# Two stage heads of a long kernel: the first attention's first operands asked for during the projection, the experts' spare rows on another queue

## The reference

```python
x = x + _L0_attn_ref(_layernorm(x), ...)
#   qkv = x @ W_attn + b_attn;  16 heads of 16
#   att = softmax(q k^T / sqrt(16) + alibi and causal mask);  y = att @ v;  y @ W_proj + b_proj
x = x + _L0_ffn_ref(...)
x = x + _L1_attn_ref(...)
x = x + _L1_ffn_ref(_layernorm(x), ...)
#   logits = xt @ w_router;  top1 = argmax;  slot = top1 * C + position, C = 160
#   buf[slot] = xt;  y = (silu(buf @ w_gate) * (buf @ w_up)) @ w_down;  out = xt + y[slot] * gate
```

## Time and profile before

| | us |
|---|---|
| median of three runs | 3570.31 (3567.07 to 3571.28) |
| the profiled execution | 3574.62 |
| span from its first to its last instruction | 3572.8 |
| PE busy in the span | 3193.6 (89%) |
| DVE, ACT, POOL busy | 2458.4, 1846.8, 1411.3 |
| mean granted TensorE clock | 0.953 |

### The profile page before, as it was taken

One profiled execution on the slowest core, in us unless ns is written; L12 is line 12 of the kernel. 1 busy time (PEld: TensorE's weight loads), 2 busy tenths in 40 slices (PEclk: granted clock), 3 DMA queues, 4 the chain that ended last, 5 costly groups with the idle time before them and its releaser, 6 DMA issues. The chain is left out here.

```text
span 3572.8 us, 52196 instructions
## 1 busy us (share of the span) xinstructions
PE 3193.6 (89%) x18048; PEld 1967.1 (55%) x18048; DVE 2458.4 (69%) x4614; ACT 1846.8 (52%) x3942; POOL 1411.3 (40%) x967
## 2 busy tenths in 40 slices
PE   8599999979999989999999899898388888888878
PEld 5244444346666645566666555433156555555777
DVE  8488887647777632277777433379699999999543
ACT  2177767736666611156666311165467777777111
POOL 4201111132222211132222211133499999999433
PEclk9699999989999999999999899999599999999989
DMA  5945657110020043000020123134444252420776
GB/s 165 168 57 91 88 86 133 35 35 23 23 66 23 14 171 99 26 19 24 22 67 21 37 68 91 48 138 149 164 170 177 82 177 86 173 93 36 260 264 219
DMA packets 263746, 347.27 MB, mean 97 GB/s; under 512 B 70619, under 2 KB 183241, under 8 KB 262844
## 3 DMA queue, kind: packets, MB, share of 16 engines
q1 hardware_dynamic: 249572, 308.29, 31.0%
q10 hardware_dynamic: 9432, 23.35, 1.9%
q0 software_dynamic: 4480, 12.30, 0.9%
HBM read 227.72 MB, written 112.80 MB: 95 GB/s over the span
## 5 line engine op out<-in xcount | busy, mean ns | idle before, releaser
L2411 POOL TENSOR_TENSOR H_feed<-H_ndu,H_bs 128x1024 f32<-128x1024 f32 x256 | 595.0, 2364 | 6.1 <-DMA H_bs<-between_bc 3.2
L888 ACT ACTIVATE B_probs<-B_p_exp,B_key_bias 128x512 f32<-128x512 f32 (+3 forms) x768 | 394.2, 582 | 161.8 <-PE B_p_exp L950 131.3
L779 DVE TENSOR_REDUCE B_part_max<-B_p_max 128x1 f32<-128x512 f32 (+3 forms) x768 | 374.3, 544 | 82.2 <-PE B_p_max L914 79.7
L1298 ACT ACTIVATE D_probs<-D_scores,D_neg,D_rq 128x256 f32<-128x256 f32 x512 | 282.9, 574 | 255.2 <-DVE D_neg L1219 255.2
L2382 ACT ACTIVATE H_decay<-H_ndt,H_rate 128x1024 f32<-128x1024 f32 x256 | 287.8, 1125 | 195.7 <-DVE H_turning L2464 103.5
L1662 PE MATMUL E_p_ag<-E_hT,FA_w 128*128 128x512 f32 x640 | 283.2, 602 | 1.9 <-ACT E_hT L1618 1.9
L911 PE MATMUL B_p_max<-B_k,B_q 100*128 100x512 bf16 (+3 forms) x768 | 256.8, 341 | 29.7 <-DMA B_q<-in_q_rows 19.7
L947 PE MATMUL B_p_exp<-B_q,B_k 100*128 100x512 bf16 (+3 forms) x768 | 250.4, 330 | 24.8 <-DMA B_q<-B_shift_rows 18.0
L2464 DVE TENSOR_TENSOR_SCAN H_turning<-H_decay,H_feed 128x1024 f32<-128x1024 f32 x112 | 253.4, 2274 | 20.6 <-POOL H_feed L2411 18.3
L2515 PEld LDWEIGHTS H_p_y<-H_minus,H_sT 128*128 128x128 f32 x1792 | 225.3, 200 | 76.0 <-ACT H_sT L2367 56.0
L2515 PE MATMUL H_p_y<-H_minus,H_sT 128*128 128x128 f32 x1792 | 233.7, 287 | 35.5 <-ACT H_sT L2367 35.5
(11 more groups left out here) (276 smaller groups left out, 6798.5 us busy)
## 6 DMA issues: line engine op xcount, KB each, us to landing
H_bs<-between_bc SPq DMA_DIRECT2D x64, 512.0 KB, 8.1
H_cs<-between_bc SPq DMA_DIRECT2D x36, 512.0 KB, 8.7
B_q<-between_q_parts SPq DMA_DIRECT2D x90, 128.0 KB
B_k<-between_k_parts SPq DMA_DIRECT2D x90, 128.0 KB
between_slots_x<-E_clear ACTq DMA_DIRECT2D x4, 2570.0 KB, 19.2
I_xe<-between_slots_x ACTq DMA_DIRECT2D x32, 257.0 KB, 6.4
LA_base<-between_z SPq DMA_DIRECT2D x64, 128.0 KB, 2.2
between_z<-D_z SPq DMA_DIRECT2D x64, 128.0 KB
```

The costliest lines, as they stand in the source:

```text
L779: nc.vector.reduce_max(part_max[:, g % 2, kc, qb, h:h + 1], p_max[:, use % 3, 0:keys], AX.X).then_inc(maxed, 1)
L888: nc.scalar.activation(probs[:, x % PROBS, skip:512], p_exp[:, n % SCORES, skip:512], ACT.Exp, bias=key_bias[:, g % SETS, kb - 4 * Q + 4, ...
L1298: last = nc.scalar.activation(probs[:, place[m], :, :].rearrange("p a b -> p (a b)"), scores[:, place[m], :, :].rearrange("p a b -> p (a b ...
L2411: nc.gpsimd.tensor_tensor(feed[:, n % AHEAD, :], ndu[:, g % 2, :], bs[:, s, :], ALU.mult).then_inc(fed, 1)
```

## The change

- A new class `FirstGroup` holds the constants and all of `q` and `k`, and is made before the projection, so that its tiles exist during both stages.
- In the projection, ACT issues four transfers (constants and position rows) in its pass for chunk 1, and three of the 12 transfers of group 0's q and k parts, 1024 columns each, in each of its passes for chunks 3 to 6, behind its wait for `qk_stored` and ahead of its L381.
- At the head of the attention these transfers are gone from SP and ACT. SP begins with group 1, then `values(0)`, then group 2. PE waits for one count of all 14. DVE makes both casts first and signals, and then fills its two tiles.
- `put_shift(0)` is issued by ACT, right behind its second L880, and no longer by SP behind group 2.
- In the experts' stage SP issues the rests of experts 0 to 3 when the scatters have landed, and those of 4 to 15 behind its waits for xe[0] to xe[5] and ahead of the weights of expert 6. ACT issues xe[0] to xe[5] first, and has run one Silu on a single column before it waits for the scatters.

```diff
@@ -376,6 +376,12 @@
...
                 reached(act, qk_stored[u], 96 * (c // 2))
+                if c == 1:
+                    first.load_fixed(act, T)
+                if PER_SEQ < c < K - 1:
+                    per = first.PARTS // (K - 2 - PER_SEQ)
+                    for n in range((c - PER_SEQ - 1) * per, (c - PER_SEQ) * per):
+                        first.load_part(act, T, n)
                 for m in range(4):
...
@@ -460,7 +466,35 @@
...
-def phase_attention(nc, T, local):
+class FirstGroup:
+    SETS, KR = 4, 100
+    PARTS = 12
+    def __init__(self, nc, ctx):
...
+        self.fixed = nc.alloc_semaphore("BF_fixed")
+        self.loaded = nc.alloc_semaphore("BF_loaded")
+    def load_fixed(self, act, T):
+        act.dma_start(self.ident[:, :], T["ident"][:, :]).then_inc(self.fixed, 16)
+        act.dma_start(self.future[:, :, :], T["future"].rearrange("a p n -> p a n")).then_inc(self.fixed, 16)
+        act.dma_start(self.k[96:self.KR, 0, :, :], T["k_rows"][0:4, :, :]).then_inc(self.loaded, 16)
+        act.dma_start(self.q[96:self.KR, 0, :, :], T["q_rows"]).then_inc(self.loaded, 16)
+    def load_part(self, act, T, n):
+        of, (x, name) = n // 2, ((self.q, "q_parts"), (self.k, "k_parts"))[n % 2]
+        at = ((0, 0), (0, 1), (1, 0), (1, 1), (0, 2), (2, 0))[of][n % 2] * SEQS * DIM
+        act.dma_start(x[HD * of:HD * of + HD, 0, :, :], T[name][at:at + GW, :].rearrange("(h d) t -> d h t", h=GH)
+                      ).then_inc(self.loaded, 16)
+def phase_attention(nc, T, local, first):
     with ExitStack() as ctx:
...
@@ -598,19 +627,6 @@
...
         def _(sp):
-            for dst, src in ((ident[:, :], T["ident"][:, :]), (future[:, :, :], T["future"].rearrange("a p n -> p a n"))):
-                sp.dma_start(dst, src).then_inc(fixed, 16)
-            def load_first():
-                for half, done in ((0, first_half), (1, second_half)):
-                    cols = slice(512 * half, 512 * half + 512)
-                    for n, part in enumerate((0, 0, 1, 1, 0, 2)):
-                        sp.dma_start(q[HD * n:HD * n + HD, 0, :, cols], T["q_parts"][part_rows(0, part), cols]
-                                     .rearrange("(h d) t -> d h t", h=GH)).then_inc(done, 16)
-                    if half == 0:
-                        sp.dma_start(q[96:KR, 0, :, :], T["q_rows"]).then_inc(done, 16)
-                values(0)
             def values(g):
...
@@ -635,10 +651,7 @@
...
                 sp.wait_ge(exped, turned[g] + 1)
-                for h in range(GH):
-                    sp.dma_start(q[96:KR, g % SETS, h, :],
-                                 shift_rows[32 * h:32 * h + 4, g % 2, :, :].rearrange("p a b -> p (a b)")
-                                 ).then_inc(q_shifted, 16)
+                move_shift(sp, g)
...
@@ -665,10 +678,9 @@
...
-            load_first()
             load(1)
+            values(0)
             load(2)
-            put_shift(0)
             sp.dma_start(w[:, :, :], T["w_proj"].rearrange("(k p) n -> p k n", p=P)).then_inc(w_loaded, 16)
...
@@ -765,9 +777,9 @@
...
             nc.vector.tensor_copy(ident_b[:, :], ident[:, :])
+            nc.vector.tensor_copy(future_b[:, :, :], future[:, :, :]).then_inc(cast, 1)
+            nc.vector.memset(part_max[:, :, 1, :, :], 4.0 * NEG)
             nc.vector.memset(shift[:, :, :, :], 0.0)
-            nc.vector.memset(part_max[:, :, 1, :, :], 4.0 * NEG)
-            nc.vector.tensor_copy(future_b[:, :, :], future[:, :, :]).then_inc(cast, 1)
             dve.drain()
...
@@ -865,19 +877,15 @@
...
         def _(act):
-            for half, done in ((0, first_half), (1, second_half)):
-                cols = slice(512 * half, 512 * half + 512)
-                for n, part in enumerate((0, 1, 0, 1, 2, 0)):
-                    act.dma_start(k[HD * n:HD * n + HD, 0, :, cols], T["k_parts"][part_rows(0, part), cols]
-                                  .rearrange("(h d) t -> d h t", h=GH)).then_inc(done, 16)
-                if half == 0:
-                    act.dma_start(k[96:KR, 0, :, :], T["k_rows"][0:4, :, :]).then_inc(done, 16)
             for n, (kind, g, at) in enumerate(stream):
...
                     nc.scalar.copy(shift_rows[:, g % 2, at, :], p_exp[:, n % SCORES, :]).then_inc(exped, 1)
+                    if g == 0 and at == 1:
+                        act.wait_ge(exped, turned[0] + 1)
+                        move_shift(act, 0)
                     continue
...
                 if n == 0:
-                    pe.wait_ge(first_half, 16 * 14)
-                if g == 0 and qb == QB // 2 and kc == 0 and h == 0:
-                    pe.wait_ge(second_half, 16 * 12)
+                    pe.wait_ge(first.loaded, 16 * (first.PARTS + 2))
                 use = max_use[n]
...
@@ -2673,6 +2679,16 @@
...
+        def load_rests(eng, f):
+            if f >= XR:
+                eng.wait_ge(xe_turned, (f - XR) * QUAD + 1)
+                eng.wait_ge(y_ready, rest_use(f - XR) + 1)
+                eng.wait_ge(rest_tokens_ready, f - XR + 1)
+            for j in range(QUAD):
+                at = (f * QUAD + j) * CAPACITY + P
+                eng.dma_start(xr[REST * j:REST * j + REST, f % XR, :], T["slots_x"][at:at + REST, :]
+                              ).then_inc(xr_loaded[f % XR], 16)
         @block.sync
...
@@ -2713,9 +2729,14 @@
...
                 store_sums(c)
+            for b in range(XB):
+                sp.wait_ge(scattered[b], 16 * CT * K // XB)
+            load_rests(sp, 0)
             sp.wait_ge(xr_loaded[0], 16 * QUAD)
...
                 sp.wait_ge(xe_loaded[b], 16)
+            for f in range(1, XR):
+                load_rests(sp, f)
             for e in range(K - 2, EXPERTS):
...
@@ -2963,16 +2974,16 @@
...
+            act.wait_ge(ones_ready, 1)
             for c in range(K):
...
                 exps(c)
+            nc.scalar.activation(sg[:, 0, 0, 0:1], ones[:, 0:1], ACT.Silu)
+            act.drain()
             for b in range(XB):
                 act.wait_ge(scattered[b], 16 * CT * K // XB)
-            load_rests(0)
             for e in range(XE - 2):
                 load_rows(e)
-            for f in range(1, XR):
-                load_rests(f)
             for e in range(EXPERTS):
...
@@ -3257,11 +3268,13 @@
...
-        phase_qkv(nc, T)
...
-            phase_attention(nc, T, local)
+            with ExitStack() as inner:
+                first = FirstGroup(nc, inner)
+                phase_qkv(nc, T, first)
+                phase_attention(nc, T, local, first)
```

More of the change, by code:

```diff
@@ L195, in normalise, with phase_qkv @@
                                        ALU.subtract, ALU.mult)
-def phase_qkv(nc, T):
+def phase_qkv(nc, T, first):
     with ExitStack() as ctx:
@@ L460, in attention_tables @@
             "key_bias": seqs(key_bias), "future": np.stack([future, future.T.copy()]), "spread": spread}
-def phase_attention(nc, T, local):
+class FirstGroup:
+    SETS, KR = 4, 100
+    PARTS = 12
+    def __init__(self, nc, ctx):
+        sb = lambda name, shape, dt=F32: ctx.enter_context(nc.sbuf_tensor(f"BF_{name}", shape, dt))
+        self.ident = sb("ident", [P, P])
+        self.future = sb("future", [P, 2, P])
+        self.q = sb("q", [P, self.SETS, GH, SEQ], BF16)
+        self.k = sb("k", [P, self.SETS, GH, SEQ], BF16)
+        self.fixed = nc.alloc_semaphore("BF_fixed")
[11 more added lines that the diff above has]
+def phase_attention(nc, T, local, first):
     with ExitStack() as ctx:
@@ L474, in phase_attention @@
         SCORES, PROBS = 3, 12
-        SETS = 4
-        KR = 100
+        SETS, KR = first.SETS, first.KR
+        ident, future, q, k, fixed = first.ident, first.future, first.q, first.k, first.fixed
         stream = [("turn", 0, 0), ("turn", 0, 1)]
@@ L490, in phase_attention @@
         tail_units = [(SEQS - 1, 2), (SEQS - 1, 3)]
-        ident = a.sb("ident", [P, P])
         ident_b = a.sb("ident_b", [P, P], BF16)
-        future = a.sb("future", [P, 2, P])
         future_b = a.sb("future_b", [P, 2, P], BF16)
-        q = a.sb("q", [P, SETS, GH, SEQ], BF16)
-        k = a.sb("k", [P, SETS, GH, SEQ], BF16)
         v_raw = a.sb("v_raw", [P, SETS, QB, GW])
@@ L523, in phase_attention @@
         p_acc = a.ps("p_acc", [P, 2, 512])
-        fixed = a.sem("fixed")
         cast = a.sem("cast")
@@ L550, in phase_attention @@
         first_row = a.sem("first_row")
-        first_half = a.sem("first_half")
-        second_half = a.sem("second_half")
         LOADED = 16 * 17
@@ L562, in loaded_by, with move_shift @@
             return LOADED * (g // SETS) + (LOADED if g % SETS else 48)
-        def part_rows(g, part):
-            at = g * GW + part * SEQS * DIM
-            return slice(at, at + GW)
+        def move_shift(eng, g):
+            for h in range(GH):
+                eng.dma_start(q[96:KR, g % SETS, h, :],
+                              shift_rows[32 * h:32 * h + 4, g % 2, :, :].rearrange("p a b -> p (a b)")
+                              ).then_inc(q_shifted, 16)
```

(11 more changed lines are left out.)

## The result

The changed kernel's median is 3560.55 us (13 runs, 3555.68 to 3568.13); the kernel before, run beside it, 3574.54 (13 runs, 3567.07 to 3578.58). The ratio is 0.9968, interval 0.9961 to 0.9975: faster by 0.32%, where 0.54% was forecast. The profiled execution of the changed kernel took 3564.5 us, its span is 3562.7 (before: 3572.8), and its granted clock 0.954 on average (before 0.953).

What follows compares the result with a forecast made beforehand. Two DMA waits of PE at the first attention's head, 19.7 and 18.0 us, were taken as the bound. 8.0 + 10.9 - 0.3 + 0.8 = 19.4 us off the median 3570.3 gave 3550.9 us, range 3545 to 3561.

Steps and rivals of the forecast that it cites:

- the cover: Attention head: values(0), with the shift computation's centre, lands at about 139, wanted at 147, so its load is hidden.
- the carrying through: Claim that everything behind the first attention's head shifts as a whole, so the gain there lasts to the span's end.
- Part 1: Attention head: operands loaded early, during the projection, bring DVE's first maximum forward; gain 8.0 us, bounds 6 and 9.2.
- Part 2: Attention head: first shift rows issued on ACT's queue, 6.4 us from copy to PE instead of 17.3; gain 10.9 us.
- L: Landing time of the first shift rows on ACT's queue beside SP's full queue, taken as 4.5 us instead of 13.8.
- the middle and the far bound: Landing of the shift rows: 4.5 us taken, near rows 2.4 and 6.6, farther bound 13.8 if the queue makes no difference.
- first rival: Attention head: shift rows land as late as before, behind the same bytes; 9.3 us less gain, 3560 us, chance 0.12.
- The sign that the prediction had set for itself: Shift rows at the attention head: the forecast for Part 2 is wrong if their landing takes above 7 us.
- Part 3: Projection: ACT's early loads are mostly hidden by its slack; 0.3 us lost, bounds 0 and 4.5.
- second and third rival: Projection: last loads paid in full, 3555 us, chance 0.09; loads delay every chunk's stores, slower at 3581 us, chance 0.03.
- Part 4: Experts' head: rests on SP, inputs first on ACT, Silu's table early; gain 0.8 us, bounds -0.5 and 2.1.
- the lower bound, -0.5: Experts' head: worst case of Part 4, if six transfers on ACT slow the rests beside them.

Runs made afterwards that it cites:

- e9: The changed kernel unaltered, timed and profiled again beside other variants: 3562.08 us, ratio 0.9971 to the kernel before.
- e7: Changed kernel with POOL's first fill of v waiting for DVE's first cast: 3563.28 us.
- e1: Changed kernel with SP holding group 2's transfers until the first shift rows have landed: 3557.06 us, ratio 0.9956 to the kernel before.
- e3: Changed kernel with the first shift rows issued by POOL behind its copy of v: 12.2 us from ACT's copy to PE.
- e6: Changed kernel with SP holding weights, bias and group 3 until the first shift rows, still on ACT's queue, have landed: 3558.05 us in one run.
- e2: Changed kernel with the first shift rows issued by SP again, behind group 2 and ahead of the weights: 3561.83 us in one run.
- e10: The same kernel as e2, timed beside the changed kernel: 3557.68 us, ratio 0.9958 to the kernel before.

## Why the prediction was partly wrong

**The direction, the cover and the carrying through were right.** Both waits at the head shrank, values(0) was there in time (POOL's copy of v at 140.90, forecast about 139, and ACT's first copy only at 148.35), and the gain at the head is still there at the end: from PE's product to the release, all 14 executions take 3260.7 to 3266.8 us, the two kernels 3262.7 and 3262.9. That spread of 6 us, with no pattern over the edits, is what blurs a comparison of single times. The granted clock has its part in it: between 1000 and 1100 us it was 1.00 in one execution of the changed kernel and 0.97 in the other (e9).

**Part 1, forecast 8.0, measured 6.6** (9.79 - 3.24). Missing are the casts: their 0.23 us was read from a row where POOL's fill had long ended, and the change put them beside it. With the fill behind the casts (e7) the part gives 8.1 (9.79 - 1.70), so this is the whole miss. The stage begins at 119.75 to 121.58 in the executions of the changed kernel and its variants, so the 1.0 us by which it came earlier in the compared pair can't be called a gain of the change.

**Part 2, forecast 10.9, measured 4.9, and not by the mechanism named: this is the step that failed.** The sum took L = 4.5 for the landing; it was 10.4, between the middle and the far bound. The argument was that ACT's queue is served beside SP's. e1, e3 and e6 show that here it isn't from the start: the rows' first packet comes only when most of what had been issued before them on q1 is done (in the changed kernel the weights have landed by then, the bias and the zeros land at about 158), and from then on they are moved side by side with q1. The first rival ("they reach the same 16 engines behind the same bytes") had the right mechanism, with a chance of 0.12. The row that was held against it, I_xe's 6.6 us beside SP's weights, shows a landing under load and not that the transfer passed anything issued ahead of it. The sign that the prediction had set for itself, L above 7, is met.

That the first rival's time, 3560, and its gain, 19.4 - 9.3 = 10.1, are so near to the 3560.55 and to the 10.1 us between the spans is luck: it has 8.0, 1.6 and 0.8 for three parts that measure 6.6, 4.9 and -1.9. The median lies within the range, by 0.45 us, because the range had been drawn to take in this rival; that doesn't bear out the sum.

The price of the part was wrong in sign as well. Against e2 and e10, which have part 1 alone, it costs 4.2 to 5.2 us. The 15.7 to 16.5 us from 53.5 to 37.8 and 37.0 are part 1's, about 6.6 of them up to the first maximum. The rest comes of SP's earlier end: with the transfers of group 0 gone from the stage, SP is through with group 2 early (e2: at 145.2, before: at 158.4), stands in its wait for 4.6 us while the DMA engines work off their load, and only then issues the rows and what follows. In the kernel before it issued them right behind group 2, without a pause; this is its last issue of group 2:

```profile
153.56 4.84 SPq L620 DMA_DIRECT2D B_key_bias<-in_key_bias  x1
```

The prediction put no price on SP's going on ("SP, freed of its wait, goes on to the weights and group 3 without a stop"). e6, which stops SP there, has 6.2 us from copy to PE where the changed kernel has 12.4. The wait that the change took away was the hold that kept the way free.

The Trainium skill has both rules ("DMA: Bandwidth & Descriptors"). "Issuing engines are not separate DMA queues" says that transfers end up on the same 16 engines and interleave, whoever issues them; the runs agree, with 12.4, 12.6 and 12.2 us for ACT's and POOL's queues. "Queues, rings and completion order" says that an engine goes round the rows packet by packet; the prediction drew from it that a small transfer gets through at once, and in this case the measurement decides against that: none of 32 packets in 149 to 156 us beside 1994 of q1. From 156 on the two queues' packets do move side by side (11 of q10 beside 73 of q1 in the microsecond from 158). Why the first come so late isn't shown.

**Part 3, forecast -0.3, measured about 0.** The stage begins at 120.70 on average over the 13 executions with the early loads, and at 120.72 in the one profile before; single ones scatter by 1.8 us. ACT issues three transfers at a time and DVE finds its tile in time:

```profile
93.06 2.42 ACT L387 ACTIVATE A_parts<-A_p_qk,A_bias_qk 128x512 bf16<-128x512 f32 x4 [8.56 <-issue]
95.65 2.05 DVE L336 SCALAR_TENSOR_TENSOR A_rest<-A_p_qk,A_bias_qk,A_parts 128x512 f32<-128x512 f32 x3
```

In 55 to 60 us the DMA share rose from 0.29 to 0.74 and PE and DVE are as full as before. The second and third rival are refuted.

**Part 4, forecast +0.8, measured -1.9.** The wait of 0.33 for hidden is gone, but nothing of it shows in the rest of the span. The 1.9 is all in PE's first turn. The fourth rest's issue starts at about 3426.0, and PE starts 5.3 us later, not 2.8: six inputs, 1.5 MB, are issued within the same 2.9 us. The 2.8 was the time of xe[0], read from a row in which the rests had gone out alone and first. This lies beyond the lower bound, -0.5.

**The sum.** 6.6 + 4.9 - 1.9 = 9.6, where 19.4 was forecast: 6.0 too much in part 2, 2.7 in part 4, 1.4 in part 1, and 0.3 too little in part 3. With the 1.0 of the earlier start and 0.4 lost in the two stretches between, these are, but for rounding, the 10.1 between the spans. The medians of all runs differ by 14.0 and the ratio makes it 11.4 (8.9 to 13.9); both are compatible with this, since single executions scatter by several us.

## What to carry to other kernels

Before moving an urgent small transfer to another queue, count what will have been issued ahead of it by all engines together, and hold the loads that nobody needs soon until it has landed: here one wait ahead of group 2 was worth 8.4 us at the place, and no later row shows a price for it beyond the scatter of 6 us. A wait that a change removes may have been the throttle on something else; write down what its engine issues in the freed time. A duration read from a row holds with the neighbours it had there; look up who will run beside it in its new place.

## What the runs showed of the hardware

- Transfers issued on an idle queue began only when most of those issued earlier on q1 were done, on ACT's and POOL's queue alike: 32 packets of q10 began in the microsecond in which q1 ran dry (e6), or after 156 us beside 65 to 90 packets of q1 per microsecond (the changed kernel). What was varied is what stood ahead and which queue carried the rows, not the kind of the rows' own transfers.
- SP's issue of one transfer can take far longer than 0.6 us under such a load. Two of the same form in the changed kernel:

```profile
126.92 0.58 SPq L635 DMA_DIRECT2D B_centre<-in_centre  x1
128.49 8.57 SPq L635 DMA_DIRECT2D B_centre<-in_centre  x1
```

- DVE's casts beside POOL's fill of 1.80 us, which had begun 0.04 us earlier, ended 0.08 and 0.21 us behind it, and took 0.23 and 0.28 us where the fill came after them (e7). The Trainium skill ("SBUF — State Buffer", "Who interferes with whom") says that the two engines share a pair of ports, and that in DVE's two-port modes, which a cast can take, the one that issues second stands still until the first is done; the runs agree.
